# A graph and linear-attention layer on one core: q and k projected ahead of v, with the edge counts at the end of q and k

## The chip, the core and the metric

The kernel is one program on 1 core of one Trainium2 chip. The metric is the device time of one execution in microseconds (us); lower is better. The core has five instruction streams that run side by side and meet only at semaphores: TensorE (PE, matrix products), VectorE (DVE), ScalarE (ACT), GpSimd (POOL) and SyncE (SP, here the issuer of nearly all DMAs). Each stream runs strictly in its own order: an instruction that waits holds back everything behind it on its engine.

## The reference, cut to what matters

```python
xn = layernorm(x)                                     # x: 1250 x 768
# graph part: three GAT layers (4 heads of 192) over 21250 + 1250 edges, all from x1
x1 = relu(xn @ W_ah + b_ah)
h = x1 @ W;  e = leaky_relu(as_n[src] + ad_n[dst], 0.2);  m = segment_max(e, dst)
p = exp(e - m[dst]);  out = segment_sum(p / s[dst] * h[src], dst) + b
x = x + relu(concat(3 x relu(out)) @ W_out + b_out)
# mixing part: linear attention, 12 heads of 64, 256 random features
q, k, v = split(xn @ w_qkv.T)
q' = ratio * (exp(q_dash - diag_q - max over the row of q_dash) + 1e-4)
k' = ratio * (exp(k_dash - diag_k - max over ALL rows, features and heads of k_dash) + 1e-4)
x = x + ((q' (k'^T v)) / (q' sum k')) @ w_proj.T + b_proj
# then a layernorm and a switch layer: 8 experts, capacity 195, 768 -> 384 -> 768
```

The greatest k_dash over everything must be known before the first exp of a k feature. The number of edges for each pair of nodes ("counts") must be known before the edge maxima.

## The kernel before, in words

The 1250 nodes lie in NT = 10 tiles of 128 rows (the last has 98). All matrix products with weights are done as three bf16 products (high and low parts), lines L911 to L913. One Python generator, `whole_order`, writes a single list ORDER of steps; every engine walks that list and does its own part of each step. Two generators are interleaved by `paced`, tick by tick: one tick of the projection and mix track (`projection_steps`, then `mix_steps`), then one tick of the graph track (`graph_steps`).

The stages around the change:

- **Scatter.** GpSimd adds the edges to three count tables in DRAM with 170 indirect DMAs (L2142), in chains of three. SyncE may load a table row only when all have landed (`tab_in`, L2256).
- **First nodes.** PE makes x1 and the h of three layers. During the third layer the six weights of v are loaded and split (`w_load` 24 to 29, `w_split` 24 to 29; high part on ACT L1867, low part on DVE L1339).
- **v.** 20 half-tiles (`v`, 18 matmuls of 384 columns each, copied by ACT L1901, written to DRAM by SP L2240).
- **q and k.** 36 products (`qk`): 12 groups n (k and q of six pairs of heads in turn, k where n is odd), each of three column chunks of 512, 512 and 226. For each: ACT Square L1911 and high part L1915 (`qk_split`), DVE L1431 and the low part L1434, PE norms L1014 and DVE L1444. During each group with odd n (it uses the k of the group before) five `k_top` steps go along: PE L1028 and a DVE maximum L1454. Every group needs a weight split.
- **Counts.** From product COUNTS_AT = 17 on the graph track is let go. Every second tick it emits `tab_in` of a tile, `count` of the tile before (DVE L1478 to L1482, then ACT copy L1920) and, two counts later, `count_turn` (PE L1066) and `absent` (DVE L1491).
- **Edge maxima.** 12 heads of 10 tiles (`edge_max`, DVE L1503), at EARLY_EDGE_RATE steps for each tick until "projected", then at other rates.
- **End of the projection.** `top_max`, `top_turn`, `top_spread` find the greatest k and make k_shift (DVE L1460 to L1471, PE L1034, L1039), with PE kept busy by `warm_mix` (L1046).
- **Mix.** Six pairs of heads, each 10 k tiles, 10 q tiles and 3 ticks: `dash` (L1102), `k_sum` (L1117, needs v of the pair from DRAM), q maxima (L1570), and so on. From the second pair on the edge work of the graph (`edge_z` L1538, exp L1931, `weigh` L1547, `gather` L1085) is interleaved. The k, v and q of pair 0 are loaded early by `pair_in` 0 (L2316 to L2325).

A product writes PSUM bank m % 3 and waits for the split of the product three before it. `k_top(i)` on PE waits for all earlier maxima on DVE.

Of the kernel before, what the change touches and what calls it, by code (L numbers as in the profile page):

```python
# [16 lines left out]
P = 128  # L17
# [36 lines left out]
NEAR = 4  # L54
HALF = NT // 2
# [12 lines left out]
COUNTS_AT = 17  # L68
COUNT_RATE, EARLY_EDGE_RATE, FIRST_EDGE_RATE, EDGE_RATE, ATTENTION_RATE = 0.5, 0.75, 1.1, (1.1, 0.5), (0.4, 0.5)
# [439 lines left out]
class Waits:  # L509
# [42 lines left out]
def program(nc, x, src_rows, dst_rows, src_cols, dst_cols, W_ah, b_ah, Wg, a_src, a_dst, bg, W_out, b_out,  # L552
            wT_qkv, wT_proj, b_proj, projT, switch_w, switch_b, w1, b1_cols, w2, b2, out):
    ctx = ExitStack()
    with ctx:
# [88 lines left out]
        absent = put("absent", [P, NT, N], BF16)  # L644
        att1 = put("att1", [P, NT, 128])
        assert cursor[0] <= r_b
# [37 lines left out]
        after_v = cursor[0]  # L684
        tab = [[put(f"tab{i}{j}", [P, N], U16) for j in range(2 + i)] for i in range(2)]
        count16 = [put(f"count16_{i}", [P, N], BF16) for i in range(2)]
        assert cursor[0] <= r_d
        cursor[0] = r_c
        k_first, q_first = put("k_first", [128, 2, N], BF16), put("q_first", [128, 2, N], BF16)
        v_first = put("v_first", [P, NT, 2, HD + 1])  # L690
        assert cursor[0] <= after_v
# [3 lines left out]
        node = [put(f"node{i}", [P, HALF, HW]) for i in range(2)]  # L695
        junk = put("junk", [P, N], BF16)
# [63 lines left out]
        tab[0].append(put("tab02", [P, N], U16))  # L760
# [25 lines left out]
        assert cursor[0] <= 229368  # L786
        cursor[0] = r_f
# [44 lines left out]
        def w_from(j):  # L832
            if j < 6:
                return W_ah[j * 128:(j + 1) * 128, :]
            if j < 24:
                l, k = divmod(j - 6, KD)
                return Wg[l][k * 128:(k + 1) * 128, :]
            if j < 30:
                k = j - 24
                return wT_qkv[k * 128:(k + 1) * 128, 2 * D:3 * D]  # L840
            n = j - 30
            c = (1 - n % 2) * D + (n // 2) * 128
            return wT_qkv[:, c:c + 128].rearrange("(k p) c -> p k c", p=128)

        def w_views(j):

            buf = stage[j % 3]
            if j < 6:
                return (buf if j < 3 else w_first[j - 3])[:, 0:D], [w[:, j, 0:D] for w in wg[0]]
            if j < 24:  # L850
                l, k = divmod(j - 6, KD)
                return buf[:, :], [w[:, k, :] for w in wg[(l + 1) % 2]]
            if j < 30:
                return buf[:, 0:D], [w[:, j - 24, :] for w in wv]
            return buf[:, 0:D].rearrange("p (k c) -> p k c", k=KD), [w[:, :, :] for w in wq[(j - 30) % 2]]
# [50 lines left out]
        def tensor_program(engine):  # L906
# [72 lines left out]
            def v(i):  # L979
                t, half = divmod(i, 2)  # L980
                R = rows(t)
                pe.wait_ge("asd_in", NT * LAYERS)
                pe.wait_ge("h_hi", NT * LAYERS)
                pe.wait_ge("v_copy", i - 2)
                cs = slice(half * HROWS, (half + 1) * HROWS)
                for k in range(KD):
                    pe.wait_ge("w_lo", 24 + k + 1)
                    ins = three(bank[i % 3][0:R, 0:HROWS], [u[:, k, at(t)] for u in xnT], [w[:, k, cs] for w in wv],
                                k == 0, k == KD - 1)
                ins.then_inc(sem["v_mm"], 1)  # L990

            def qk(m, part):
                n = m // NC
                c0, c1 = chunk(m)
                r = 2 * NT + m
                if m < 3:
                    pe.wait_ge("v_copy", r - 2)
                pe.wait_ge("qk_lo", m - 2)
                pe.wait_ge("w_lo", 30 + n + 1)
                for k in range(part * KD // 2, (part + 1) * KD // 2):  # L1000
                    ins = three(bank[r % 3][:, 0:c1 - c0], [w[:, k, :] for w in wq[n % 2]],
                                [u[:, k, c0:c1] for u in xnT], k == 0, k == KD - 1)
                if part:
                    ins.then_inc(sem["qk_mm"], 1)
# [44 lines left out]
            def warm_mix(n):  # L1049
                pe.wait_ge("qk_lo", NC * 2 * PAIRS)  # L1050
                keep_warm(0, n)
# [18 lines left out]
            def gather(i):  # L1070
                lh, half, pair = item(i)
                H = i // SPLITS
                pe.wait_ge("qk_lo", NC * 2 * PAIRS)
# [201 lines left out]
        def vector_program(engine):  # L1275
# [150 lines left out]
            def qk_split(m):  # L1426
# [7 lines left out]
                V.scalar_tensor_tensor(dst[:, 1, c0:c1], bank[(2 * NT + m) % 3][:, 0:c1 - c0], NORM, dst[:, 0, c0:c1],  # L1434
# [391 lines left out]
        def scalar_program(engine):  # L1826
# [31 lines left out]
            def w_split(j):  # L1858
                buf, parts = w_views(j)
                se.wait_ge(*w_count(j))  # L1860
                if 24 <= j < 30:
                    se.wait_ge("h_mm", 2 * NT * (LAYERS - 1))
                if j >= 32:
                    se.wait_ge("qk_mm", NC * (j - 31))
                if j == 30:
                    se.wait_ge("feats_hi", 1)
# [27 lines left out]
            def v(i):  # L1894
# [7 lines left out]
                             bank[i % 3][0:R, 0:HROWS].rearrange("p (a h c) -> p a h c", h=2, c=HD),  # L1902
                             ACT.Copy).then_inc(sem["v_copy"], 1)

            def qk_split(m):
                n = m // NC
                c0, c1 = chunk(m)
                b = bank[(2 * NT + m) % 3][:, 0:c1 - c0]
# [282 lines left out]
        def sync_program(engine):  # L2191
# [12 lines left out]
            def w_load(j):  # L2204
                sy.wait_ge("w_lo", j - 5 if j < 9 else j - 2)
                S.dma_start(w_views(j)[0] if j >= 24 else stage[j % 3][:, 0:D], w_from(j)).then_inc(sem[w_count(j)[0]], 16)
# [41 lines left out]
            def tab_in(t):  # L2248
                R = rows(t)
                sy.wait_ge("h_mm", 2 * NT * LAYERS)  # L2250
                sy.wait_ge("h_out2", 16 * (NT * LAYERS // 3))
                for i in range(TABLES):
# [49 lines left out]

            def pair_in(pair):
                i = pair % 2
                if pair == 0:
                    sy.wait_ge("v_mm", 2 * NT)
                else:
                    sy.wait_ge("qk_mm", NC * 2 * PAIRS)
                for j in range(2):
                    sy.wait_ge(f"qk_out{j}", 16 * (PAIRS if pair else 1))  # L2310
                    sy.wait_ge(f"v_out{j}", 16 * HALF)
# [6 lines left out]
                full, rest = by_tiles(v_rows[pair], 0, NT)  # L2318
                vv = values_of(pair)[:, :, :, :].rearrange("p t h c -> p t (h c)")
                S.dma_start(vv[:, 0:FULL, :], full).then_inc(sem[f"v_in{i}"], 16)  # L2320
                S.dma_start(vv[0:LAST, FULL, :], rest).then_inc(sem[f"v_in{i}"], 16)
# [103 lines left out]
            def own_(t):  # L2425
# [5 lines left out]
                        head_in=head_in, finish=finish, pair_in=pair_in, divide=divide,  # L2431
# [55 lines left out]
```

## Time and profile before

| | us |
|---|---|
| median of 3 runs | 1708.28 (1707.54 to 1710.41) |
| the profiled execution, its own time | 1709.37 |
| its span on the core | 1707.6 |
| mean granted clock of TensorE | 0.962 of full speed |

The rows of the section below come from this one profiled execution. A timeline row gives the start (us from the span's start), the duration, the engine, the line and the operation, and in brackets how long the engine had been idle and what ended that.

### The profile page before, as it was taken

Reading aid. Unit: us, or ns where it says so; the run is one execution under the profiler, and the core shown is the slowest. Engines: PE = TensorE matmul, PEld = TensorE weight load, DVE = VectorE, ACT = ScalarE, POOL = GpSimd, SP = SyncE. Lnnn points to the kernel's source line nnn. Section 1 sums busy time; section 2 is a strip of 40 time slices with the busy share of each in tenths; the row PEclk is TensorE's granted clock in tenths of the full one; section 3 lists DMA queues with packets and bytes.
Section 4 is the critical chain, followed back from the end, with each engine's and each line's share of the span. In section 5 each row is a group of like instructions: output and inputs, shape, how many; then the busy total and the mean of one; then the engine's idle time right before and its main releaser. Section 6 shows DMA issues by size and latency. Waiting matters only on the chain.

```text
span 1707.6 us, 25848 instructions
## 1 busy us (share of the span) xinstructions
PE 1541.5 (90%) x10083; PEld 1186.8 (70%) x10109; DVE 1149.2 (67%) x2629; ACT 681.4 (40%) x1359; POOL 410.1 (24%) x251
## 2 busy tenths in 40 slices
PE   3989999999878789998999989998999999986987
PEld 2556666555444568988888988888888976656664
DVE  6677664105567989999987787668766833885323
ACT  3420001122233366877777763346434621441110
POOL 3688888888500000000000000000000000002331
PEclk9989999999989899999999999999999999986999
DMA  9435545464752514324420354236413224545951
GB/s 342 97 64 113 111 84 122 71 93 75 190 187 87 143 42 120 88 90 114 125 71 28 104 166 162 96 126 197 129 38 103 82 68 153 213 181 203 319 158 50
DMA packets 196620, 213.72 MB, mean 125 GB/s; under 512 B 81551, under 2 KB 149789, under 8 KB 196498
## 3 DMA queue, kind: packets, MB, share of 16 engines
q1 hardware_dynamic: 119874, 187.01, 34.6%
q0 software_dynamic: 75760, 22.70, 8.8%
q10 hardware_dynamic: 864, 2.36, 0.4%
q8 instruction: 80, 1.31, 0.3%
q14 instruction: 42, 0.34, 0.1%
HBM read 144.74 MB, written 68.40 MB: 125 GB/s over the span
## 4 chain that ended last, share of the span: by engine, by line
PE 45%; DVE 19%; POOL 17%; DMA 9%; issue 7%; ACT 3%; SPq 1%; POOLq 0%; ACTq 0%; DVEq 0%
PE bank L1085 17%; POOL table L2142 17%; DVE junk L1503 5%; PE bank L913 4%; PE bank L911 4%; PE bank L912 4%; PE bank L1261 4%; DMA table<-amount,place 3%; PE bank L1249 3%; DVE eb L1538 2%; DVE eb L1547 2%; PE bank L1145 2%; DMA table<-zero 2%; PE bank L1117 1%; PE bank L1102 1%
## 5 line engine op out<-in xcount | busy, mean ns | idle before, releaser
L1085 PE MATMUL bank<-hb,eb 128*128 128x193 f32 (+3 forms) x2400 | 418.8, 332 | 14.5 <-ACT node L1945 9.2
L1085 PEld LDWEIGHTS bank<-hb,eb 128*128 128x128 f32 (+3 forms) x2400 | 399.5, 191 | 20.6 <-issue 10.5
L2142 POOL DMA_INDIRECT table<-amount,place x170 | 345.2, 2030 | 74.4 <-issue 49.1
L2148 POOL IOTA iota8i<- 128x8 int32 x1 | 0.1, 140 | 941.7 <-DMA node_rows<-node 941.7
L1538 DVE SCALAR_TENSOR_TENSOR eb<-shift_b,as_low,shift_b 128x640 f32<-128x640 f32 (+1 forms) x240 | 196.4, 860 | 0.3 <-PE bank L1085 0.2
L1931 ACT ACTIVATE eb<-eb,asd 128x640 f32<-128x640 f32 (+1 forms) x240 | 181.5, 812 | 28.9 <-DVE eb L1538 28.9
L1547 DVE SCALAR_TENSOR_TENSOR eb<-eb,count 128x1280 f32<-128x1280 f32 (+1 forms) x120 | 174.6, 1455 | 2.3 <-ACT eb L1931 2.3
L1503 DVE CUSTOM_DVE_ANT_0 junk<-ab,absent 128x1250 bf16<-128x1250 f32 x120 | 174.3, 1453 | 1.5
L911 PE MATMUL bank<-w_o_hi,aT_hi 128*128 128x384 bf16 (+1 forms) x360 | 119.1, 331 | 0.0
L911 PE MATMUL bank<-wg_hi,x1T_hi 128*128 128x384 bf16 (+3 forms) x360 | 118.9, 330 | 0.1
L913 PE MATMUL bank<-w_o_hi,aT_lo 128*128 128x384 bf16 (+1 forms) x360 | 119.0, 330 | 0.0
L912 PE MATMUL bank<-w_o_lo,aT_hi 128*128 128x384 bf16 (+1 forms) x360 | 118.9, 330 | 0.0
L912 PE MATMUL bank<-wg_lo,x1T_hi 128*128 128x384 bf16 (+3 forms) x360 | 118.8, 330 | 0.0
L913 PE MATMUL bank<-wg_hi,x1T_lo 128*128 128x384 bf16 (+3 forms) x360 | 118.8, 330 | 0.0
L912 PE MATMUL bank<-xnT_lo,wq_hi 128*128 128x512 bf16 (+1 forms) x212 | 74.9, 353 | 4.6 <-DVE wq_lo L1339 3.0
L1377 DVE TENSOR_TENSOR h_row<-bank,bgr 128x384 f32<-128x384 f32 (+1 forms) x60 | 32.5, 555 | 64.8 <-PE bank L913 64.7
L913 PE MATMUL bank<-xnT_hi,wq_lo 128*128 128x512 bf16 (+1 forms) x215 | 75.8, 352 | 0.2
L1803 DVE TENSOR_TENSOR orow<-bank,b2r 105x384 f32<-105x384 f32 (+1 forms) x32 | 17.8, 555 | 82.8 <-PE bank L1261 82.8
L1970 ACT ACTIVATE ef<-bank,q_shift 128x256 f32<-128x256 f32 (+1 forms) x120 | 50.5, 473 | 51.2 <-DVE q_shift L1575 51.0
L911 PE MATMUL bank<-xnT_hi,wq_hi 128*128 128x512 bf16 (+1 forms) x201 | 70.8, 352 | 0.1
L1877 ACT ACTIVATE wg_hi<-stage 128x776 bf16<-128x776 f32 x18 | 15.3, 850 | 135.5 <-DVE stage L1353 135.5
L1945 ACT ACTIVATE node<-bank 128x386 f32<-128x386 f32 (+1 forms) x72 | 29.3, 442 | 88.3 <-PE bank L1085 88.3
(280 smaller groups left out, 2965.9 us busy)
## 6 DMA issues: line engine op xcount, KB each, us to landing
w<-in_w SPq DMA_DIRECT2D x16, 1152.0 KB, 12.5
shift_b<-shift_rows SPq DMA_DIRECT2D x24, 625.0 KB, 5.8
h_rows<-h_row SPq DMA_DIRECT2D x27, 388.0 KB
hb<-h_rows SPq DMA_DIRECT2D x12, 873.0 KB
ar<-node_rows SPq DMA_DIRECT2D x27, 384.0 KB
table<-zero POOLq DMA_DIRECT2D x3, 3054.0 KB, 21.7
tab<-table SPq DMA_DIRECT2D x27, 312.5 KB, 3.6
qk_rows<-qk_row SPq DMA_DIRECT2D x12, 625.0 KB
```

The lines of the kernel that those rows point to most:

```text
L911: T.matmul(out_ap, lhs[0], rhs[0], start=first, stop=False, skip_group_check=skip)
L912: T.matmul(out_ap, lhs[0], rhs[1], start=False, stop=False, skip_group_check=skip)
L913: return T.matmul(out_ap, lhs[1], rhs[0], start=False, stop=last, skip_group_check=skip)
L1085: ins = T.matmul(bank[w // 2][0:M, c0:c0 + GC + 1], p[0:K, u, w * P:w * P + M], hv[0:K, t, 0:GC + 1], start=opens and u == 0 and w % 2 == ...
L1249: ins = T.matmul(bank[i % 2][:, 0:CAP], w1s[e % WEIGHT_SETS][:, k, f * 128:(f + 1) * 128], sT_of(k)[:, e * CAP:(e + 1) * CAP], start=k == ...
L1261: ins = T.matmul(bank[4 + i % 4][0:r1 - r0, 0:HROWS], hT[e % 2][:, f, r0:r1], w2s[e % WEIGHT_SETS][:, f, cs], start=f == 0, stop=f == KF - 1)
L1503: V.tensor_tensor_reduce(out=junk[0:R, :], in0=ab[lh % 2][0:R, :], in1=absent[0:R, t, :], scale=1.0, scalar=-BIG, op0=ALU.add, op1=ALU.max ...
L1538: ins = V.scalar_tensor_tensor(eb[i % EDGE_BUFFERS][:, u, 0:w], low, as_low[:, t, lh:lh + 1], high, ALU.add, ALU.max)
L1547: V.scalar_tensor_tensor(e, e, 1.0, count[:, 2 * pair:2 * pair + 2, ns], ALU.min, ALU.mult).then_inc(sem["edge_w"], 1)
L1931: ins = A.activation(e[:, u, 0:w], e[:, u, 0:w], ACT.Exp, bias=asd[:, t, 8 * l + hh:8 * l + hh + 1])
L1970: ins = A.activation(ef[g % 4][0:R, hh, :], bank[3 + g % 2][0:R, hh * FEATS:(hh + 1) * FEATS], ACT.Exp, bias=bias)
L2142: G.indirect_dma_start(tables[i], bass.IndirectOffsetOnAxis(place[:, c:c + 1], axis=0), amount16[:, c:c + 1], None, compute_op=ALU.add).th ...
```

## The change

q and k are projected first and v last. The weights get new numbers (q and k 24 to 35, v 36 to 41); the v weights are loaded and split at the end of q and k. COUNTS_AT becomes 27. The edge maxima's early rate becomes 1.6 per tick. The chain of the greatest k goes behind half-tiles 1, 3 and 5 of v and `warm_mix` of that place goes. The values of pair 0 are loaded by a step of its own behind v. Some buffers move.

```diff
+FIRST_QK, FIRST_V = 24, 36
-COUNTS_AT = 17
-COUNT_RATE, EARLY_EDGE_RATE, FIRST_EDGE_RATE, EDGE_RATE, ATTENTION_RATE = 0.5, 0.75, 1.1, (1.1, 0.5), (0.4, 0.5)
+COUNTS_AT = 27
+COUNT_RATE, EARLY_EDGE_RATE, FIRST_EDGE_RATE, EDGE_RATE, ATTENTION_RATE = 0.5, 1.6, 1.1, (1.1, 0.5), (0.4, 0.5)
...
             if l + 1 == LAYERS:
-                if 0 <= t - 1 < KD:
-                    yield "w_load", 24 + t - 1
-                if 0 <= t - 2 < KD:
-                    yield "w_split", 24 + t - 2
+                if 1 <= t < 3:
+                    yield "w_load", FIRST_QK + t - 1
+                if t == 3:
+                    yield "w_split", FIRST_QK
...
 def projection_steps(done):
     yield "feats_in", 0
-    for t in range(NT):
-        for half in range(2):
-            yield "v", 2 * t + half
-            yield None
-        if t >= NT - 2:
-            yield "w_load", 30 + t - NT + 2
-    yield "w_split", 30
 
     def product(m):
         n, c = divmod(m, NC)
         if m == COUNTS_AT:
             done.add("scattered")
         if c == 0 and n + 2 < 2 * PAIRS:
-            yield "w_load", 30 + n + 2
+            yield "w_load", FIRST_QK + n + 2
...
             if part == 0 and c == 0 and n + 1 < 2 * PAIRS:
-                yield "w_split", 30 + n + 1
+                yield "w_split", FIRST_QK + n + 1
+            k = m - NC * 2 * PAIRS + KD + 1
+            if part == 0 and 0 <= k <= KD:
+                if k < KD:
+                    yield "w_load", FIRST_V + k
+                if k:
+                    yield "w_split", FIRST_V + k - 1
...
-    yield "top_max", 0
-    yield "warm_mix", 8
-    yield None
-    yield "top_turn", 0
-    yield "warm_mix", 4
-    yield None
-    yield "top_spread", 0
-    yield "warm_mix", 6
+    for i in range(2 * NT):
+        yield "v", i
+        if i in (1, 3, 5):
+            yield ("top_max", "top_turn", "top_spread")[i // 2], 0
+        yield None
+    yield "values_in", 0
     done.add("projected")
-    yield None
...
             def v(i):
                 t, half = divmod(i, 2)
                 R = rows(t)
-                pe.wait_ge("asd_in", NT * LAYERS)
-                pe.wait_ge("h_hi", NT * LAYERS)
+                r = NC * 2 * PAIRS + i
+                if i < 3:
+                    pe.wait_ge("qk_lo", r - 2)
                 pe.wait_ge("v_copy", i - 2)
...
+            def values_in(pair):
+                for j in range(2):
+                    sy.wait_ge(f"v_out{j}", 16 * HALF)
+                full, rest = by_tiles(v_rows[pair], 0, NT)
+                vv = values_of(pair)[:, :, :, :].rearrange("p t h c -> p t (h c)")
+                S.dma_start(vv[:, 0:FULL, :], full).then_inc(sem[f"v_in{pair % 2}"], 16)
+                S.dma_start(vv[0:LAST, FULL, :], rest).then_inc(sem[f"v_in{pair % 2}"], 16)
+
             def pair_in(pair):
                 i = pair % 2
-                if pair == 0:
-                    sy.wait_ge("v_mm", 2 * NT)
-                else:
-                    sy.wait_ge("qk_mm", NC * 2 * PAIRS)
+                if pair:
+                    sy.wait_ge("qk_mm", NC * 2 * PAIRS)
+                    sy.wait_ge("v_mm", 2 * NT)
                 for j in range(2):
                     sy.wait_ge(f"qk_out{j}", 16 * (PAIRS if pair else 1))
-                    sy.wait_ge(f"v_out{j}", 16 * HALF)
...
-                full, rest = by_tiles(v_rows[pair], 0, NT)
...
+                if pair:
+                    values_in(pair)
```

## Rows read from the trace of the kernel before

**Rows 1.** the page, part 1: share of the span and busy time by engine
```profile
PE 1541.5 (90%) x10083; PEld 1186.8 (70%) x10109; DVE 1149.2 (67%) x2629; ACT 681.4 (40%) x1359; POOL 410.1 (24%) x251
```

**Rows 2.** one stretch: busy time by engine, granted clock, DMA share, GB/s
```profile
460.00:480.00 20.00, 14.01 (x96) 8.15 (x96) 12.23 (x25) 6.91 (x10) 0.00 (x0) 0.83 0.89 303
```

**Rows 3.** timeline: last scatter, first table load, first count (start us, us, work)
```profile
453.36 1.99 POOL L2142 DMA_INDIRECT table<-amount,place  x1 [0.30 <-issue]
457.23 1.27 SPq L2256 DMA_DIRECT2D tab<-table  x3
462.13 0.81 DVE L1478 TENSOR_TENSOR count<-tab,tab 128x1250 uint16<-128x1250 uint16 x1 [5.50 <-DMA tab<-table]
```

**Rows 4.** line L2142, ns min/median/max: beside idle VectorE, then beside busy VectorE
```profile
L2142 POOL DMA_INDIRECT table<-amount,place x23: 1988/1992/2012, 320.1 to 370.6; - x23
...
L2142 POOL DMA_INDIRECT table<-amount,place x17: 1988/1993/2637, 389.8 to 428.0; - x17
```

**Rows 5.** timeline: first matmul of product 0, then Square of products 5 and 17
```profile
376.79 0.38 PE L912 MATMUL bank<-xnT_lo,wq_hi 128*128 128x512 bf16 x1 [2.96 <-DVE wq_lo L1339]
...
401.92 0.36 ACT L1911 ACTIVATE sq<-bank 128x226 f32<-128x226 f32 x1 [2.95 <-PE bank L913]
...
452.58 0.36 ACT L1911 ACTIVATE sq<-bank 128x226 f32<-128x226 f32 x1 [2.95 <-PE bank L913]
```

**Rows 6.** timeline, ScalarE: copies of counts 0, 1, 3, 5, 6 and 7 of ten
```profile
464.15 1.25 ACT L1920 ACTIVATE count<-count 128x1250 bf16<-128x1250 uint16 x1 [10.24 <-DVE count L1482]
...
469.21 1.25 ACT L1920 ACTIVATE count<-count 128x1250 bf16<-128x1250 uint16 x1 [2.84 <-DVE count L1482]
...
482.65 1.25 ACT L1920 ACTIVATE count<-count 128x1250 bf16<-128x1250 uint16 x1 [4.98 <-DVE count L1482]
...
501.45 1.25 ACT L1920 ACTIVATE count<-count 128x1250 bf16<-128x1250 uint16 x1 [6.97 <-DVE count L1482]
...
507.77 1.25 ACT L1920 ACTIVATE count<-count 128x1250 bf16<-128x1250 uint16 x1 [3.85 <-DVE count L1482]
...
513.69 1.25 ACT L1920 ACTIVATE count<-count 128x1250 bf16<-128x1250 uint16 x1 [3.70 <-DVE count L1482]
```

**Rows 7.** timeline, VectorE: a weight split and a maximum of k
```profile
477.70 0.96 DVE L1339 TENSOR_TENSOR wq_lo<-stage,wq_hi 128x768 bf16<-128x768 f32 x1 [0.28 <-ACT wq_hi L1867]
...
478.65 1.21 DVE L1454 TENSOR_REDUCE kmax<-bank 128x1 f32<-128x1024 f32 x1
```

**Rows 8.** timeline, ScalarE: copies of v, half-tiles 1 and 19 of 0 to 19
```profile
321.22 0.49 ACT L1901 ACTIVATE v_row<-bank 128x384 f32<-128x384 f32 x1 [2.37 <-PE bank L913]
...
373.87 0.49 ACT L1901 ACTIVATE v_row<-bank 98x384 f32<-98x384 f32 x1 [2.37 <-PE bank L913]
```

**Rows 9.** us from issue to landing: v_rows written (L2240), k_first read, ab read
```profile
DMA to landing us min/median/max: 4.4/4.6/5.4
...
DMA to landing us min/median/max: 4.9/5.3/5.8
...
ab<-as_rows SPq DMA_DIRECT2D x1, 625.0 KB, 8.2
```

**Rows 10.** timeline: start of the mix: first k_sum, first q maximum
```profile
581.93 0.52 PE L1117 MATMUL bank<-v_first,ef 128*128 128x65 f32 x3 [2.20 <-issue]
...
599.96 0.69 DVE L1570 TENSOR_REDUCE q_max<-bank 128x2 f32<-128x512 f32 x1 [1.98 <-PE bank L1102]
```

**Rows 11.** edge maxima before the mix (ns); a stretch of 40 us behind it
```profile
L1503 DVE CUSTOM_DVE_ANT_0 junk<-ab,absent x12: 1419/1453/1462, 545.1 to 577.7; 128x1250 bf16<-128x1250 f32 x11, 98x1250 bf16<-98x1250 f32 x1
...
880.00:920.00 40.00, 37.52 (x262) 36.33 (x262) 37.36 (x64) 28.11 (x68) 0.00 (x0) 0.91 0.28 85
```

**Rows 12.** timeline, SP: store of the finished pair 3, 4 and 5
```profile
838.59 0.39 SPq L2332 DMA_DIRECT2D attn_rows<-att  x1
...
907.78 0.39 SPq L2332 DMA_DIRECT2D attn_rows<-att  x1
...
974.30 0.37 SPq L2332 DMA_DIRECT2D attn_rows<-att  x1
```

More of the change, by code:

```diff
@@ L644, in program @@
         absent = put("absent", [P, NT, N], BF16)
+        at_att1 = cursor[0]
         att1 = put("att1", [P, NT, 128])
+        assert cursor[0] <= r_b
+        cursor[0] = at_att1
+        tab = [[put(f"tab0{j}", [P, N], U16) for j in range(2)], []]
         assert cursor[0] <= r_b
@@ L683, in program @@
         wv = [put(f"wv_{p}", [128, KD, D], BF16) for p in ("hi", "lo")]
[L684 to L688, printed above, removed]
         k_first, q_first = put("k_first", [128, 2, N], BF16), put("q_first", [128, 2, N], BF16)
         v_first = put("v_first", [P, NT, 2, HD + 1])
-        assert cursor[0] <= after_v
+        after_first = cursor[0]
+        count16 = [put("count16_0", [P, N], BF16)]
+        assert cursor[0] <= r_d
         cursor[0] = r_c
@@ L695, in program @@
         node = [put(f"node{i}", [P, HALF, HW]) for i in range(2)]
+        cursor[0] = after_first
         junk = put("junk", [P, N], BF16)
@@ L759, in program @@
         cursor[0] = r_f - size([P, N], U16)
-        tab[0].append(put("tab02", [P, N], U16))
+        count16.append(put("count16_1", [P, N], BF16))
         cursor[0] = r_e
@@ L786, in program @@
         assert cursor[0] <= 229368
+        cursor[0] -= 2 * size([P, N], F32)
+        tab[0].append(put("tab02", [P, N], U16))
+        tab[1] += [put(f"tab1{j}", [P, N], U16) for j in range(2)]
+        assert cursor[0] <= after
+        cursor[0] = r_f
+        tab[1].append(put("tab12", [P, N], U16))
         cursor[0] = r_f
@@ L837, in w_from @@
                 return Wg[l][k * 128:(k + 1) * 128, :]
-            if j < 30:
-                k = j - 24
+            if j >= FIRST_V:
+                k = j - FIRST_V
                 return wT_qkv[k * 128:(k + 1) * 128, 2 * D:3 * D]
-            n = j - 30
+            n = j - FIRST_QK
             c = (1 - n % 2) * D + (n // 2) * 128
@@ L852, in w_views @@
                 return buf[:, :], [w[:, k, :] for w in wg[(l + 1) % 2]]
-            if j < 30:
-                return buf[:, 0:D], [w[:, j - 24, :] for w in wv]
-            return buf[:, 0:D].rearrange("p (k c) -> p k c", k=KD), [w[:, :, :] for w in wq[(j - 30) % 2]]
+            if j >= FIRST_V:
+                return buf[:, 0:D], [w[:, j - FIRST_V, :] for w in wv]
+            return buf[:, 0:D].rearrange("p (k c) -> p k c", k=KD), [w[:, :, :] for w in wq[(j - FIRST_QK) % 2]]
         def out_from(jj):
@@ L986, in v @@
                 for k in range(KD):
-                    pe.wait_ge("w_lo", 24 + k + 1)
-                    ins = three(bank[i % 3][0:R, 0:HROWS], [u[:, k, at(t)] for u in xnT], [w[:, k, cs] for w in wv],
+                    pe.wait_ge("w_lo", FIRST_V + k + 1)
+                    ins = three(bank[r % 3][0:R, 0:HROWS], [u[:, k, at(t)] for u in xnT], [w[:, k, cs] for w in wv],
                                 k == 0, k == KD - 1)
@@ L994, in qk @@
                 c0, c1 = chunk(m)
-                r = 2 * NT + m
-                if m < 3:
-                    pe.wait_ge("v_copy", r - 2)
+                pe.wait_ge("asd_in", NT * LAYERS)
+                pe.wait_ge("h_hi", NT * LAYERS)
                 pe.wait_ge("qk_lo", m - 2)
-                pe.wait_ge("w_lo", 30 + n + 1)
+                pe.wait_ge("w_lo", FIRST_QK + n + 1)
                 for k in range(part * KD // 2, (part + 1) * KD // 2):
-                    ins = three(bank[r % 3][:, 0:c1 - c0], [w[:, k, :] for w in wq[n % 2]],
+                    ins = three(bank[m % 3][:, 0:c1 - c0], [w[:, k, :] for w in wq[n % 2]],
                                 [u[:, k, c0:c1] for u in xnT], k == 0, k == KD - 1)
@@ L1049, in warm_mix @@
             def warm_mix(n):
-                pe.wait_ge("qk_lo", NC * 2 * PAIRS)
+                pe.wait_ge("v_copy", 2 * NT)
                 keep_warm(0, n)
@@ L1072, in gather @@
                 H = i // SPLITS
-                pe.wait_ge("qk_lo", NC * 2 * PAIRS)
+                pe.wait_ge("v_copy", 2 * NT)
                 pe.wait_ge("edge_w", i + 1)
@@ L1860, in w_split @@
                 se.wait_ge(*w_count(j))
-                if 24 <= j < 30:
+                if j >= FIRST_V:
                     se.wait_ge("h_mm", 2 * NT * (LAYERS - 1))
[L1863 to L1866, printed above, removed]
+                elif j >= FIRST_QK + 2:
+                    se.wait_ge("qk_mm", NC * (j - FIRST_QK - 1))
+                elif j == FIRST_QK:
+                    se.wait_ge("turned", 2 * NT)
                 A.activation(parts[0], buf, ACT.Copy).then_inc(sem["w_hi"], 1)
@@ L1907, in qk_split @@
                 c0, c1 = chunk(m)
-                b = bank[(2 * NT + m) % 3][:, 0:c1 - c0]
+                b = bank[m % 3][:, 0:c1 - c0]
                 se.wait_ge("qk_mm", m + 1)
@@ L2205, in w_load @@
                 sy.wait_ge("w_lo", j - 5 if j < 9 else j - 2)
-                S.dma_start(w_views(j)[0] if j >= 24 else stage[j % 3][:, 0:D], w_from(j)).then_inc(sem[w_count(j)[0]], 16)
+                S.dma_start(w_views(j)[0] if j >= FIRST_QK else stage[j % 3][:, 0:D], w_from(j)).then_inc(sem[w_count(j)[0]], 16)
             def w_part(p):
@@ L2251, in tab_in @@
                 sy.wait_ge("h_out2", 16 * (NT * LAYERS // 3))
+                sy.wait_ge("as_rows_out", 16)
                 for i in range(TABLES):
@@ L2317, in pair_in @@
                                 qk_rows[1, pair][:, s, :].rearrange("(h d) n -> d h n", h=2)).then_inc(sem[f"k_in{i}"], 16)
-                full, rest = by_tiles(v_rows[pair], 0, NT)
-                vv = values_of(pair)[:, :, :, :].rearrange("p t h c -> p t (h c)")
-                S.dma_start(vv[:, 0:FULL, :], full).then_inc(sem[f"v_in{i}"], 16)
-                S.dma_start(vv[0:LAST, FULL, :], rest).then_inc(sem[f"v_in{i}"], 16)
+                if pair:
+                    values_in(pair)
                 if pair >= 2:
@@ L2430, in sync_program @@
                         feats_in=feats_in, v=v, qk_store=qk_store, tab_in=tab_in, ab_in=ab_in, shift_store=shift_store,
-                        head_in=head_in, finish=finish, pair_in=pair_in, divide=divide,
+                        head_in=head_in, finish=finish, pair_in=pair_in, values_in=values_in, divide=divide,
                         mix_bias=mix_bias, out_load=out_load, row_in=row_in, x_in2=x_in2,
```

4 lines of the change are left out of this document (2 added, 2 removed), and 2 rows, old and new, of the table TAKEN_OVER.

## The prediction, made before the changed kernel was run

> **What bounds the kernel now.** I read the page first: PE is busy 90% of the span, DVE 67%, POOL 24% [rows 1]. That is an average over stages with different limits, so I went on to the stretches of 20 us, the chain of waits, and then the timelines of POOL, SP, ACT and DVE from 310 to 635 us, which is where the diff works. Three things are to be seen there.
>
> First, a fixed point: the last scatter is issued at 453.36, SyncE loads the first table rows at 457.23 and DVE, idle for 5.5 us, makes count 0 at 462.13 [rows 3]. GpSimd is paced by its own issue, about 2.3 us for each of 170 scatters (1.99 us of work and 0.30 us between them [rows 3]), so whatever PE does earlier, the counts can't start before this point. Second, behind it PE isn't full: 14.0 us busy of 20, at a mean granted clock of 0.83 of full speed [rows 2]. There DVE and ACT pass each product and each count through in turn. Third, from the mix on DVE sets the pace while edge maxima remain (37.36 of 40 us busy), with PE close behind (37.52) [rows 11].
>
> So the question is how much work stands behind the fixed point before the mix can start, and how much DVE work is then still to do. What is done before the point is free if it fits.
>
> **The order.** I count the ticks of the two tracks from the start of the projection. Before, v has ticks 0 to 19 and product m begins at tick 20 + 2m, so product 17 is at tick 54. After, product m begins at tick 2m, so product 27 is at tick 54 too. Count j is at tick 57 + 2j either way: before, count 0 stands ahead of the split of product 18, after, ahead of the split of product 28.
>
> **When PE gets there.** Before, product 0 starts at 376.79 and product 17 ends at 452.58; products 6 to 17 take 452.58 - 401.92 = 50.7 us [rows 5]. Thirty products therefore take 75.8 + 50.7 = 126.5 us. The projection starts two half-tiles ahead of the copy at 321.22; a half-tile takes (373.87 - 321.22) / 18 = 2.93 us [rows 8], so it starts at about 315. PE then ends product 29 at about 441. It can't go on: k_top 24 waits for a maximum that DVE has behind count 0. Queued behind the waiting count are, on DVE, all splits, norms and maxima, and behind `tab_in` on SP the store of group 8 and the weight loads of v. DVE reaches count 0 by about 434 and waits 28 us for 462.13 [rows 3]. Before, the same wait cost it 5.5 us. PE stands still from 441 to about 468.
>
> Does the scatter end sooner, as v's stores no longer run beside it? The work of a scatter is 1.992 us beside v and 1.993 us beside q and k [rows 4], and its few waits for landings near 440 come from the loads of pair 0, which move to about 376. I give that 0 to 4 us and take 0. The Trainium skill, "GPSIMD Engine Reference", section "Key points", speaks against the change here: GpSimd shares its SBUF interfaces with VectorE, with contention beside DVE instructions that have two SBUF inputs. In the new order DVE is busy beside 27 scatters beside which it was idle. The rows don't show a cost (same median), only single long ones.
>
> **The counts' stretch.** I add up the intervals between the ACT copies of the counts. With nothing else an interval is 469.21 - 464.15 = 5.06 us; with the absent part 513.69 - 507.77 = 5.92, so that part is 0.86; with the absent part and two k_top steps, whose PE part can't be hidden, (501.45 - 482.65) / 2 = 9.40 [rows 6]. A weight split adds 0.28 + 0.96 = 1.24 [rows 7]. A product of 226 columns is 0.6 shorter (the difference of such a split to a full one, an estimate); a single k_top adds the 1.14 of its maximum (1.21 less the overlap with its neighbour [rows 7]). The six v splits fall in here, one for each product from 30 to 35. They were hidden in the third layer, where DVE had time; so removing them there gains nothing, and here they stand in the chain. Intervals after count 0: 8.5 (two k_top, no absent part yet), 7.8, 7.2, 7.2, 7.7, 10.6, 10.6: together 59.6 us. From 464.15 [rows 6] that is 523.8 for count 7, and 2.3 more for the split of product 35, which the last norms wait for: v starts at about 526. Before, the same ten counts stood beside ten products with 3 weight splits. If the v splits find gaps this is 7 us less; if PE's clock stays low, up to 4 us more.
>
> **v behind the point.** 20 x 2.93 = 58.5 us [rows 8], and about 2 us for the last three `count_turn` on PE: v ends at 587. Counts 8 and 9 and the last absents hide beside it, and so does the chain of the greatest k: it needs a few short steps on DVE and two on PE. Before, that chain with its warm matmuls was between the last product and the mix; gone.
>
> **The turnaround through DRAM.** This is an added wait. k_sum 0 needs v of all rows of pair 0. The copy of the last half-tile takes 0.49 [rows 8], its store 4.4 to 5.4 to land [rows 9], then `values_in` issues two loads (1.3) that land after a time which before doesn't show alone. Nearest rows: 5.3 for half the bytes, 8.2 for slightly more [rows 9]; the packets are small but few, so I take 5.3, and keep 8.2. Sum: 0.5 + 4.6 + 1.3 + 5.3 = 11.7, so k_sum 0 at 587 + 11.7 = 598.7. Without the wait it would come about 4 us behind the first dash, so 7.5 us are exposed. Behind it on PE stand all further dashes; ACT, and at the first q maximum DVE, wait in turn. The Trainium skill, "DMA: Bandwidth & Descriptors", section "Anatomy of one DMA", gives a DMA as 2.0 us and its bytes at 436 GB/s; an estimate by that page for both transfers is 6.0 us in place of 9.9, and the sum below would be 4 us smaller. Our row of 4.6 us for 390 KB, where the page gives 2.9, is why I don't use it.
>
> Before, k_sum 0 was at 581.93 and the first q maximum followed 18.0 us later [rows 10]. That stage isn't changed. So the mix starts 598.7 - 581.93 = **16.8 us later**.
>
> **What comes back.** By the first dash DVE had made 12 maxima [rows 11]; after, 15 ticks x 1.6 = 24 are emitted before "projected", and they fit beside v (15 x 2.93 = 44 us for 24 x 1.5 = 36 us). At the emitted counts (18 x 0.75 gives 13) DVE is 11 maxima ahead, 16.6 us of its work. What is that worth? Between 838.59 and 907.78 the pair of heads with maxima took 69.2 us; the last, 907.78 to 974.30, almost free of them, took 66.5 [rows 12]. PE takes over as the bound almost at once. Eleven maxima are about half a pair's, so I take 2 us back (0 to 5). Behind 1000 us PE is full and passes all on.
>
> **Sum.** +16.8 - 2 = +14.8. On the profiled execution that is 1709.4 + 14.8 = 1724.2 (span 1707.6 + 14.8 = 1722.4); the median of the runs is 1.1 lower: 1708.3 + 14.8 = **1723**. Its own range is 1716 to 1731.
>
> **The rivals.**
> - *The v splits and the DMAs are cheap.* The splits find gaps (-7) and the scatter ends 3 us sooner. For it: DVE waits 1.8 us or so for ACT in each interval. Against: each engine is in order, and the splits stand ahead of the next count. 14.8 - 10 = +5: 1713.
> - *The lead of the maxima is paid in full.* This is the one that ends on the other side, not slower. DVE is 93% busy from the mix to the last maximum [rows 11]; if it alone is the bound, 11 maxima give back 16.6 us and the sum is 0: 1708. It decides where a pair without maxima is more than 15 us shorter than one with them; the rows show 2.7 [rows 12]. With the cheap splits on top it would be 1708 - 8 = 1700, faster.
> - *DVE slows the scatters.* If the 27 scatters beside which DVE was idle took as long as the worst beside a busy DVE (2.64 in place of 1.99 [rows 4]), the fixed point moves by 27 x 0.65 = 17 us: 1740. This is what the cited rule on shared interfaces would do at worst. The equal medians speak against it.
>
> **How the numbers follow.** Chances: forecast 0.62, cheap splits 0.15, lead paid in full 0.13, the same and faster 0.07, slowed scatters 0.03. A measurement of this kernel can tell about 0.2%, 3.4 us, from no change: 1704.9 to 1711.7. Faster is the fourth case, 0.08 with rounding; same is the third and a little of the second, 0.16; the rest, 0.76, is slower. From 1707 to 1731 the range takes in the first three cases and both ends of the unknown costs; left out are the two far ones and the overshoot of the forecast.
>
> **What would show it.** In the new profile: DVE idle for 20 us and more ahead of L1478 count 0, and that at 458 to 463; PE idle from about 441; ACT copies of the counts 7 to 11 us apart; the last v copy at 583 to 590; PE waiting 6 to 10 us for a DMA ahead of its first k_sum, and DVE some 15 to 20 us ahead of the first q maximum; the last edge maximum earlier relative to the mix than before. It would be wrong if the scatters ended near 440 (then PE has no gap), if DVE didn't wait at count 0, or if pairs with maxima became much shorter.

## The result and the profile after

The changed kernel takes 1729.49 us in the median of 4 runs (1728.94 to 1729.77), the kernel before 1709.35 (1707.54 to 1713.24) beside it: ratio 1.0107 [1.0082, 1.0131]. It is 1.1% slower. In the profiled executions the span grows from 1707.6 to 1728.0, by 20.4 us. The prediction had the sign and the mechanism; its sum was +14.8.

Busy times hardly move against [rows 1] (PE's falls by 9 us); the 20.4 us are standing time.

```profile
PE 1532.2 (89%) x10091; PEld 1183.7 (68%) x10091; DVE 1152.0 (67%) x2629; ACT 680.6 (39%) x1359; POOL 414.3 (24%) x251
```

The timeline of after at the fixed point (start us, us, work; in brackets the idle time before and what ended it), for POOL, SP and DVE. It answers to [rows 3]: all three come later, and DVE has been idle for 33 us, where it was 5.5.

```profile
457.93 1.99 POOL L2147 DMA_INDIRECT table<-amount,place  x1 [0.30 <-issue]
...
461.88 1.29 SPq L2262 DMA_DIRECT2D tab<-table  x3
...
467.74 0.81 DVE L1483 TENSOR_TENSOR count<-tab,tab 128x1250 uint16<-128x1250 uint16 x1 [33.05 <-DMA tab<-table]
```

The same view on PE: the last matmul of product 29, and the next one, a `k_top` that waits for a maximum queued on DVE behind count 0.

```profile
436.44 0.26 PE L918 MATMUL bank<-xnT_hi,wq_lo 128*128 128x226 bf16 x1
474.00 0.39 PE L1033 MATMUL bank<-feats_hi,qk_row 64*128 64x256 bf16 x2 [37.30 <-DVE kmax L1459]
```

Stretches of 20 us of after: busy PE, PEld, DVE, ACT and POOL, then TensorE's granted clock, DMA share, GB/s. In the first nothing works but POOL. [Rows 2] had 14.01 us of PE where the second row has 6.00.

```profile
440.00:460.00 20.00, 0.00 (x0) 0.00 (x0) 0.00 (x0) 0.00 (x0) 17.48 (x9) 0.51 0.19 1
460.00:480.00 20.00, 6.00 (x35) 2.86 (x36) 7.58 (x13) 3.50 (x5) 0.00 (x0) 0.55 0.64 219
480.00:500.00 20.00, 14.67 (x108) 7.98 (x106) 15.22 (x32) 8.24 (x13) 0.00 (x0) 0.91 0.72 233
```

ScalarE's copies of counts 0, 1 and 7 of ten, as in [rows 6]: from count 0 to count 7 it is 58.96 us.

```profile
469.75 1.25 ACT L1925 ACTIVATE count<-count 128x1250 bf16<-128x1250 uint16 x1 [41.79 <-DVE count L1487]
478.72 1.25 ACT L1925 ACTIVATE count<-count 128x1250 bf16<-128x1250 uint16 x1 [6.75 <-DVE count L1487]
...
528.71 1.25 ACT L1925 ACTIVATE count<-count 128x1250 bf16<-128x1250 uint16 x1 [7.75 <-DVE count L1487]
```

The timeline at the turnaround through DRAM: the last copy of v, the two loads of `values_in`, the first `k_sum`, the first q maximum. The last two answer to [rows 10] and come 20.6 and 21.4 us later.

```profile
594.35 0.49 ACT L1906 ACTIVATE v_row<-bank 98x384 f32<-98x384 f32 x1 [2.37 <-PE bank L918]
...
598.17 0.36 SPq L2314 DMA_DIRECT2D v_first<-v_rows  x1
598.57 0.60 SPq L2315 DMA_DIRECT2D v_first<-v_rows  x1
...
602.56 1.97 PE L1122 MATMUL bank<-v_first,ef 128*128 128x65 f32 x8 [5.76 <-DMA v_first<-v_rows]
...
621.35 0.69 DVE L1575 TENSOR_REDUCE q_max<-bank 128x2 f32<-128x512 f32 x1 [4.78 <-PE bank L1107]
```

And the end of the mix: the last edge maximum, and the store of pair 5. The store is 21.8 us later than in [rows 12], so nearly nothing has come back.

```profile
922.50 1.45 DVE L1508 CUSTOM_DVE_ANT_0 junk<-ab,absent 98x1250 bf16<-98x1250 f32 x1
...
996.10 0.37 SPq L2342 DMA_DIRECT2D attn_rows<-att  x1
```

### The profile page after: what moved, and what is told of

The parts are those of the page before. It is cut to its first block, busy times and chain, and to the rows that moved or that the text cites. A ratio compares the mean times of both kernels' runs of the same rounds, so it can differ in the third digit from the quotient of the medians.

```text
span 1728.0 us, 25838 instructions
## 1 busy us (share of the span) xinstructions
PE 1532.2 (89%) x10091; PEld 1183.7 (68%) x10091; DVE 1152.0 (67%) x2629; ACT 680.6 (39%) x1359; POOL 414.3 (24%) x251
## 4 chain that ended last, share of the span: by engine, by line
PE 50%; POOL 17%; DVE 16%; DMA 7%; issue 6%; ACT 4%; SPq 0%; POOLq 0%; ACTq 0%; DVEq 0%
PE bank L1090 18%; POOL table L2147 17%; PE bank L916 5%; PE bank L917 5%; PE bank L918 5%; DMA table<-amount,place 4%; PE bank L1266 4%; DVE junk L1508 3%; PE bank L1254 3%; PE bank L1150 2%; DVE eb L1543 2%; PE bank L1122 2%; PE bank L1107 2%; DVE eb L1552 1%; PE bank L1165 1%
## 5 line engine op out<-in xcount | busy, mean ns | idle before, releaser
L2147 POOL DMA_INDIRECT table<-amount,place x170 | 349.2, 2054 | 75.2 <-issue 49.0
L916 PE MATMUL bank<-xnT_hi,wq_hi 128*128 128x512 bf16 (+1 forms) x216 | 74.9, 347 | 0.0
L1033 PE MATMUL bank<-feats_hi,qk_row 64*128 64x256 bf16 (+1 forms) x240 | 27.3, 290 | 51.0 <-DVE kmax L1459 48.4
```

Source lines behind the costliest of these rows:

```text
L916: T.matmul(out_ap, lhs[0], rhs[0], start=first, stop=False, skip_group_check=skip)
L2147: G.indirect_dma_start(tables[i], bass.IndirectOffsetOnAxis(place[:, c:c + 1], axis=0), amount16[:, c:c + 1], None, compute_op=ALU.add).th ...
```

## The experiments

The theory: everything that stands behind the end of the scatters and ahead of the mix costs its full time, and what stands ahead of it is free. The rivals: TensorE's stop itself is harmless; the late scatters, the DRAM turnaround or the lead of the edge maxima explain the 20 us. The kernel before was timed beside every group of runs (medians 1709.35, 1713.95, 1715.43), so kernels of different groups are compared by their ratios to it. Each timeline, and each number read from one, is of a single profiled execution.

**More products ahead of the counts.** Only the place of the counts, eight products later.

```diff
-COUNTS_AT = 27
+COUNTS_AT = 35
```

> The changed kernel with COUNTS_AT = 35 in place of 27, nothing else. Theory (what costs is the work that the order puts behind the end of the scatter): product 35 ends about 25 us behind product 29, at 462, just as the tables are there; DVE waits only a few us at count 0; the ten counts then stand beside v, where ACT and DVE have time, and not beside six products. v from 462 to about 535 (20 x 2.93 and ten count_turns of 1.3 us), the first k_sum at 540 to 548 in place of 602.6, so 55 to 62 us earlier. The counts end at tick 96, so no edge maximum is made before the mix (24 in the changed kernel): about one more pair of heads with maxima, 3 to 6 us back. Time 1668 to 1682 us. Rival (DVE is the bound of the mix, the lead of maxima counts in full): 24 x 1.5 = 36 us back, time 1705 to 1712. Rival (the counts slow v as they slowed the products, 6 us each): the first k_sum at about 560, time 1690.

Measured: 1676.47 us (1673.39 to 1679.55), ratio 0.9784 [0.9761, 0.9806], faster than before by 2.2%. The scatters ended later still (461.76), and the kernel is 53 us faster than with 27 by the medians, 55 by the ratios. The first `k_sum` came at 540.07, as expected. The timeline of DVE, and two stretches, show why: DVE waits 6 us instead of 33, and PE is busy through the end of the scatters and fully busy behind it, where v runs and DVE has room for the counts.

```profile
471.18 0.81 DVE L1483 TENSOR_TENSOR count<-tab,tab 128x1250 uint16<-128x1250 uint16 x1 [6.00 <-DMA tab<-table]
...
558.42 0.69 DVE L1575 TENSOR_REDUCE q_max<-bank 128x2 f32<-128x512 f32 x1 [12.10 <-PE bank L1107]
```

```profile
440.00:460.00 20.00, 19.65 (x167) 10.86 (x166) 13.54 (x24) 8.61 (x15) 15.06 (x9) 1.00 0.71 176
...
480.00:500.00 20.00, 20.00 (x144) 12.69 (x143) 7.74 (x20) 6.24 (x9) 0.00 (x0) 1.00 0.89 225
```

**Half way.**

```diff
-COUNTS_AT = 27
+COUNTS_AT = 31
```

> COUNTS_AT 31 in the changed kernel, everything else as it is. Theory (each product that stands behind the fixed point of the scatters costs its whole interval, each one ahead of it is free): COUNTS_AT 27 gave 1729.5 us and 35 gave 1676.5, so 53 us for eight products, 6.6 each. TensorE should reach its stop at about 449, stand still some 20 us instead of 37, and the time should lie half way, 1699 to 1707. Rival (TensorE has to be held up at all for the loss to come, a step rather than a slope; 31 still ends its products before the scatters end): 1720 or more. Rival (the ten counts cost nothing once more than half lie beside v): 1685 or less.

Measured: 1702.93 us (1699.24 to 1706.57), ratio 0.993 [0.9907, 0.9953]. The three ratios are 1.0107, 0.993 and 0.9784 for 27, 31 and 35: about 30 and 25 us for four products each, a slope and no step. PE stood still for 18.4 us, and DVE's wait at count 0 halves:

```profile
467.83 0.81 DVE L1483 TENSOR_TENSOR count<-tab,tab 128x1250 uint16<-128x1250 uint16 x1 [17.04 <-DMA tab<-table]
```

**Late counts in the old order.** The kernel before with the counts at product 27, v still first.

```diff
-COUNTS_AT = 17
+COUNTS_AT = 27
```

> The kernel before (v first, q and k last) with COUNTS_AT 27 in place of 17, nothing else. It separates the place of the counts from the order of q, k and v. Theory (it is the order that makes late counts pay, since VectorE is idle beside v and busy beside q and k): here the counts only move from one group of q and k products to another, beside which VectorE is just as busy; the 5.5 us of waiting at count 0 go, the twelve maxima ahead of the mix go too, the last two counts fall behind the products. Within 6 us of the kernel before, ratio 0.995 to 1.003. Rival (late counts are better in any order): ratio 0.985 or less. The wait at count 0 should be under 1 us and its start near 495.

Measured: 1712.04 us (1709.25 to 1715.16), ratio 0.9984 [0.997, 0.9999]. So late counts alone bring next to nothing. The reason was only half foreseen. On the timeline of DVE count 0 waits for nothing, and the mix does begin 8.3 us earlier than in [rows 10]; but with few maxima ahead of it the last one comes at 978.88 (before: 918.47), and the store of pair 5 stands where it stood [rows 12]. Whether a higher early rate would keep these 8.3 us in the old order was not run. The gain with 35 is over four times as much, and the experiments show it only with v behind the counts.

```profile
499.37 0.80 DVE L1478 TENSOR_TENSOR count<-tab,tab 128x1250 uint16<-128x1250 uint16 x1
...
591.70 0.69 DVE L1570 TENSOR_REDUCE q_max<-bank 128x2 f32<-128x512 f32 x1 [8.39 <-PE bank L1102]
...
974.10 0.37 SPq L2332 DMA_DIRECT2D attn_rows<-att  x1
...
978.88 1.46 DVE L1503 CUSTOM_DVE_ANT_0 junk<-ab,absent 98x1250 bf16<-98x1250 f32 x1
```

**The turnaround by itself.** ScalarE copies the values of pair 0 straight into their buffer, beside the copy that goes to DRAM.

```diff
-    yield "values_in", 0
...
+                if half == 0:
+                    A.activation(v_first[0:R, t, :, 0:HD],
+                                 bank[(NC * 2 * PAIRS + i) % 3][0:R, 0:2 * HD].rearrange("p (h c) -> p h c", h=2), ACT.Copy)
```

> The changed kernel with the values of pair 0 copied by ACT straight from PSUM into their buffer beside the copy for DRAM (ten copies of 128 columns more), so the first k_sum waits for no DMA; COUNTS_AT stays 27. Theory by the changed kernel's trace: the first feature is ready at 598.9, the first k_sum came at 602.6, so 3.7 us are to be had, less some 0.3 for the added copies: 1725.5 to 1727. Rival (the 7.5 us that the prediction gave to the turnaround): 1722. Rival (the wait is hidden, the first q maxima are held by something else): 1729.5.

Measured: 1724.94 us (1723.94 to 1728.17), ratio 1.0067 [1.0045, 1.0089]. The first q maximum came 6.1 us earlier (615.25) and the span was 5.8 us shorter (1722.2). But not all of this is the turnaround: the last copy of v came 1.8 us earlier too (592.58 against 594.35). From that copy to the first q maximum it is 22.7 us where after has 27.0, so the turnaround is worth 4.3 us of the 20. That is near the 3.7 of the theory; the rival of 7.5 falls.

**The lead of the maxima.** The early rate as it was before.

```diff
-COUNT_RATE, EARLY_EDGE_RATE, FIRST_EDGE_RATE, EDGE_RATE, ATTENTION_RATE = 0.5, 1.6, 1.1, (1.1, 0.5), (0.4, 0.5)
+COUNT_RATE, EARLY_EDGE_RATE, FIRST_EDGE_RATE, EDGE_RATE, ATTENTION_RATE = 0.5, 0.75, 1.1, (1.1, 0.5), (0.4, 0.5)
```

> The changed kernel with the early rate of the edge maxima back at 0.75 per tick: 11 maxima before the mix in place of 24. Theory (PE takes over as the bound as soon as DVE has less to do, a maximum moved from the mix to the projection is worth some 0.1 us): +1 to +3 us, 1730.5 to 1732.5. Rival (the lead counts in full): 13 x 1.5 = 19.5 us, 1749.

Measured: 1729.74 us (1725.79 to 1734.82), ratio 1.009 [1.0059, 1.012]: the interval holds the changed kernel's ratio. In the profile 20 maxima were made ahead of the first q maximum, after has 32. Twelve more or less can't be seen in the time, and the rival (the lead counts in full) falls.

**What makes a scatter long.** The low part of the squares is a copy from PSUM instead of a difference of two SBUF operands; the norms are therefore not the reference's, and DVE also waits for ScalarE's high part.

```diff
-                V.tensor_tensor(sq_parts[m % 3][:, 0:w, 0], sq[m % 3][:, 0:w], sq_parts[m % 3][:, 0:w, 1],
-                                ALU.subtract).then_inc(sem["square_lo"], 1)
+                ve.wait_ge("qk_hi", m + 1)
+                V.tensor_copy(sq_parts[m % 3][:, 0:w, 0], bank[m % 3][:, 0:w]).then_inc(sem["square_lo"], 1)
```

> The changed kernel with the low part of the squares of q and k left out: in its place DVE copies the product from PSUM, one input in PSUM in place of two in SBUF, so the norms (and the output) are not the reference's; all else is the same. Theory (DVE instructions with two SBUF inputs lengthen the scatters that they meet): the long scatters that met only a square split become 1.99 us, those that meet a weight split stay long; the last scatter is issued at 455 to 456.5 in place of 457.9 and the time is 1.5 to 3 us less. Rival (it is DMA traffic or anything that DVE does): the scatters stay as long, 457.9.

Measured, one execution: 1735.62 us, the last scatter at 458.61, so the expected time and the expected end of the scatters were both missed. The scatters themselves did what the theory says. The view of line L2147 (ns min/median/max) from 376 us on, of after and then of this kernel:

```profile
L2147 POOL DMA_INDIRECT table<-amount,place x35: 1987/1993/2819, 374.8 to 457.9; - x35
```

```profile
L2147 POOL DMA_INDIRECT table<-amount,place x35: 1988/1992/2012, 377.9 to 458.6; - x35
```

The long ones are gone (from 2819 ns to 2012 at most), so the difference of two SBUF operands on DVE does stretch a scatter. (Between 300 and 376 us two long ones of 31 are left, at 326.85 and 367.20, each with the low part of a weight beside it, which this kernel still makes as a difference; after had 7 there.) The saving is there as well, once the scatters are compared by their number and not by the time. This profile reached the 113th of the 170 scatters 4.3 us later than after did, ahead of anything that the edit touches (the first Square at 319.20, after: 316.72). From there to the last it took 138.7 us where after took 142.2, that is 3.6 us less.

The whole was slower for another reason. Count 0 is copied at 469.76, level with after (469.75), but count 7 comes 2.7 us later (531.46): the edit makes DVE wait for ScalarE's high part, and between 480 and 530 us DVE's waits for ScalarE at this step grew from 10.3 to 13.2 us. The other 3.2 us of the 5.9 by which the span is longer lie behind the first q maximum and are not settled.

**The two good edits together.** COUNTS_AT 35 with the direct values of above.

> COUNTS_AT 35 and the values of pair 0 copied by ScalarE straight into their buffer, so the two edits that gave 1676.5 and, beside COUNTS_AT 27, 4.6 us less than the changed kernel. Theory (the turnaround through DRAM lies on the path in both): the first q maximum 5 to 7 us ahead of the 558.4 of the run with COUNTS_AT 35 alone, and 1669 to 1674. Rival (with COUNTS_AT 35 the maxima and counts still queued on VectorE take up what the turnaround gives back): 1675 to 1678.

Measured: 1676.76 us (1668.31 to 1680.67), ratio 0.9769 [0.974, 0.9797], against 0.9784 without: no difference that can be told. The time is the rival's, not the theory's, and the first q maximum came at 558.23, level with 558.42 and not 5 to 7 us ahead. In its profile the last copy of v came at 535.57 (counts at 35 alone: 531.52) and the first q maximum 22.7 us behind it instead of 26.9. So the turnaround gave 4.2 us, and v was 4.1 us later; of those, 3.1 were there at the first product already (318.96, 315.86). Whether the direct values are worth anything here stays open.

**Counts twice as fast.** The same with a count in every tick.

```diff
-COUNT_RATE, EARLY_EDGE_RATE, FIRST_EDGE_RATE, EDGE_RATE, ATTENTION_RATE = 0.5, 1.6, 1.1, (1.1, 0.5), (0.4, 0.5)
+COUNT_RATE, EARLY_EDGE_RATE, FIRST_EDGE_RATE, EDGE_RATE, ATTENTION_RATE = 1.0, 1.6, 1.1, (1.1, 0.5), (0.4, 0.5)
```

> As the run with COUNTS_AT 35 and direct values, and a count in every tick instead of every second one. Theory (a count takes ScalarE and VectorE about 5 us, a half-tile of v 2.9, so counts at twice the rate hold the copies of v up; but the maxima behind them start sooner): v ends 0 to 5 us later, more maxima are made ahead of the mix, and the lead in maxima is worth under 1 us by the run with the slower maxima: same as the run at the slow rate within 3 us, 1669 to 1676. Rival (VectorE sets the pace of the mix and the lead is paid): 1660 or less.

Measured: 1682.62 us (1680.32 to 1684.88), ratio 0.9813 [0.9792, 0.9835], some 6 us worse than at the slow rate. Both the expected time and the expected end of v were missed. The last copy of v came at 552.02, 16.5 us later and not 0 to 5: a count needs far more of DVE and ScalarE than a half-tile of v leaves free. The 21 maxima that were made in that time brought back 6 us (expected: under 1) of the 15 by which the first q maximum was late (573.28 against 558.23).

The profiles together price the lead. For each kernel: maxima made ahead of the first q maximum, and the time from that to the store of pair 5.

| kernel | maxima | us to the store |
|---|---|---|
| before | 24 | 374.3 |
| changed | 32 | 374.8 |
| changed, direct values | 32 | 374.3 |
| changed, early rate 0.75 | 20 | 375.4 |
| COUNTS_AT 31 | 19 | 372.2 |
| COUNTS_AT 35 | 8 | 376.3 |
| COUNTS_AT 35, direct values | 8 | 379.9 |
| the same, count rate 1.0 | 29 | 374.1 |
| before, COUNTS_AT 27 | 7 | 382.4 |

The kernel without the square's difference is left out, as its edit costs DVE time of its own. From 19 maxima on the lead is worth nothing; at 7 or 8 its lack costs 2 to 8 us.

## Why the prediction was right, and where its sum was short

**The stop.** Right. PE was to end product 29 at 441 and stand until about 468, DVE to wait 28 us. It was 436, 474 and 33 us. The place of PE's stop costs nothing in itself, since the end is set by the fixed point; what a standing PE costs behind it is told under v.

**The fixed point: the term that was mis-sized.** I took 0, with 0 to 4 us sooner. The last scatter came 4.6 us later and count 0 5.6 us later (467.74, [rows 3]); the last 1.0 us came with the load of the table rows. I argued from equal medians [rows 4]. A median doesn't see a few long ones. Where q and k now run beside scatters that had v beside them, the view shows scatters of up to 2646 ns, where [rows 4] has 2012 at most:

```profile
L2147 POOL DMA_INDIRECT table<-amount,place x22: 1989/1994/2646, 318.0 to 371.5; - x22
```

The timeline shows what they meet. POOL, then DVE, of after:

```profile
342.69 1.99 POOL L2147 DMA_INDIRECT table<-amount,place  x1 [0.30 <-issue]
345.59 2.52 POOL L2147 DMA_INDIRECT table<-amount,place  x1 [0.91 <-DMA table<-amount,place]
348.42 2.57 POOL L2147 DMA_INDIRECT table<-amount,place  x1 [0.30 <-issue]
```

```profile
345.54 0.75 DVE L1436 TENSOR_TENSOR sq<-sq 128x512 bf16<-128x512 f32 x1 [2.43 <-ACT sq L1916]
...
348.16 0.96 DVE L1344 TENSOR_TENSOR wq_lo<-stage,wq_hi 128x768 bf16<-128x768 f32 x1 [0.28 <-ACT wq_hi L1872]
```

Each long scatter has the low part of a square or of a weight beside it, both differences of two SBUF operands. From 300 us on 29 of after's scatters overlap such a difference; 13 of these took more than 2.02 us, and none of the 36 others did. The rule that I had weighed, the Trainium skill, "GPSIMD Engine Reference", section "Key points", holds in kind. The run without the square's difference shows the cause.

How much of the 4.6 us this makes can be read by the scatters' numbers. The table adds up POOL's timeline from the start of the 113th scatter, where before and after are level to 0.2 us, to the start of the 170th, the last.

| kernel | 113th starts at | us to the 170th | work in them | waits for a landing |
|---|---|---|---|---|
| before | 315.5 | 137.9 | 116.2 | 5.8 |
| before, COUNTS_AT 27 | 318.4 | 141.3 | 118.6 | 6.4 |
| changed | 315.7 | 142.2 | 119.7 | 6.7 |
| changed, no square's difference | 320.0 | 138.7 | 114.5 | 7.6 |

Of the 4.4 us in this stretch 3.5 are longer scatters and 0.9 are waits. These are balances of gains and losses. The loss falls mainly between the 113th and the 139th, where DVE was idle before: 60.0 and 60.8 us in the two profiles of the old order, 64.4 to 66.7 in all eight of the new one. After lost 6.0 us there: 3.5 by longer scatters and 3.2 by more waits for landings, less 0.6 of other idle time. Without the square's difference the scatters are only 0.9 longer, and the waits 4.0. What causes these waits no run separates. Up to the 157th after loses 3.2 us more, and behind it wins 4.9 back: 1.5 of work, since DVE stands idle there, and 4.0 of waits, since those near 442 are gone.

The kernel before with COUNTS_AT 27 warns against more exactness. It has the old order, and again none long beside v:

```profile
L2142 POOL DMA_INDIRECT table<-amount,place x25: 1988/1992/2012, 316.1 to 371.4; - x25
```

Yet its last scatter starts at 459.76, 6.4 us later than before's 453.36 [rows 3]: it was 2.9 us late at the 113th already, and three of its last scatters, from 448 us on, were long where before had none. So one profile of before wasn't enough to take 453.36 as given, and the range should have carried that term upwards as well.

**The counts' stretch.** Predicted 59.6 us, measured 58.96. The single intervals agree too, so this is not two errors that cancel: 8.97, 7.19, 6.80, 6.87, 7.79, 10.64 and 10.70 us, where the sum had 8.5, 7.8, 7.2, 7.2, 7.7, 10.6 and 10.6. So the v splits did stand in the chain; the rival of cheap splits falls.

**v.** Its end was predicted at 587; the last copy is at 594.35. Of the 7.4 us, 5.6 are the fixed point. The other 1.8 are TensorE's clock. v starts at 531.38, which is the 526 of the sum and the 5.6; but its first half-tile takes 5.1 us instead of 2.93, at a granted clock of 0.51 from 531 to 536 us. Ahead of that PE had been busy for 3.9 of the 10 us from 520 to 530, at 0.61. In the next 5 us the clock was 1.00, and the same matmul took 0.33 us instead of 0.53. The 2 us that I gave to the last `count_turn` steps came as counted.

```profile
535.17 0.53 PE L916 MATMUL bank<-wv_hi,xnT_hi 128*128 128x384 bf16 x1
...
537.05 0.33 PE L916 MATMUL bank<-wv_hi,xnT_hi 128*128 128x384 bf16 x1
```

**The turnaround.** Predicted 11.7 us from v to the first `k_sum`; measured from the last copy 602.56 - 594.35 = 8.2. From the end of that copy to the loads it is 3.3 us, where I took 4.6 for the store, and from the second load to the matmul 4.0, where I took 5.3. The estimate by the Trainium skill, "DMA: Bandwidth & Descriptors", section "Anatomy of one DMA", 6.0 us for both transfers, was nearer than my rows (7.3 against 9.9). But that section gives its figures for DMAs that GpSimd issues, and SyncE issued these, so this one case doesn't bear them out. Predicted were 7.5 us exposed. PE waits 5.8 us at `k_sum`, and the run without the turnaround gives 4.3.

**What comes back.** Predicted 2 us. The first q maximum is 21.4 later, the store of pair 5 21.8, the end 20.4: 0 to 1 us. One part was counted wrongly: against the first q maximum, where DVE becomes the bound, the lead grew from 24 maxima to 32, by 8 and not by 11, since before DVE made twelve more during its first k tiles. The rival in which the lead is paid in full falls with the run at the slow rate.

**The sum.** +16.8 became +20.6 at the first `k_sum` (7.4 more from v's end, 3.5 less from the turnaround), -2 became about 0. That is the 20.4 of the span. The two large errors pulled in opposite directions, a fixed point that came later and a turnaround that was shorter; that the time stayed inside the range, 1.5 us below its upper end, is in part luck.

**The place of the counts.** The order of the change was not at fault, its COUNTS_AT was. With v last, each product of q and k between 27 and 35 is worth some 6 to 7 us ahead of the fixed point; at 35 the same order is 2.2% faster than before. My working named what is done ahead of the point as free, but followed only the one setting.

## What to carry to other kernels

When a stage waits for something that comes at a fixed time, list what stands behind it and what fits ahead of it, and move the work with the shortest chain behind it (here v, which leaves VectorE idle for the counts) to the far side; an idle engine just ahead of the fixed point is the room that is left. Read the sum over the stretch in question, and not the median of a group, before saying that a neighbour doesn't disturb it; the mean over all 170 scatters would not have done either (2030 ns before, 2054 after, but 2052 in the old order with COUNTS_AT 27). Compare two profiles of a chain by the number of its links, so that a late start isn't taken for a slow stretch. A lead on the engine that is busiest later is worth something only up to the point where another becomes the bound.

## What the hardware showed that wasn't expected

A scatter's issue of 1.99 us on GpSimd took up to 2.82 us when VectorE made a difference of two SBUF operands beside it, and 2.01 at most where it did not (36 scatters of after from 300 us on, and the 23 and 25 beside v in the two kernels of the old order). Not every such difference did it: of the 29 scatters of after that overlap one, 16 stayed at 2.01 or less, and in 15 of these the difference began 0.4 us or more into the scatter. In 10 of the 13 long ones it was already running or began together with the scatter; the other three met two differences within their first 1.0 us.

TensorE, which had stood still from 436 us on, had a granted clock of 0.51 in the stretch from 440 to 460, about the lower of its two levels (1.2 of 2.4 GHz), and 0.55 in the next. The first matmuls behind the stop show it on the timeline: four of them took 0.63 us together, where the same four took 0.38 just ahead of the stop.

```profile
434.98 0.38 PE L1033 MATMUL bank<-feats_hi,qk_row 64*128 64x256 bf16 x4
...
474.40 0.63 PE L1033 MATMUL bank<-feats_hi,qk_row 64*128 64x256 bf16 x4
```
